# Halved queries, keys and gates in passes 1 to 3 of a fused attention and mixture-of-experts block

## The chip, the cores and the metric

The kernel runs on one core of a Trainium2 chip. The metric is the device time of one execution in microseconds (us). The core has five engines that run side by side, each with an instruction queue of its own: TensorE (PE; its weight loads are shown apart as PEld), VectorE (DVE), ScalarE (ACT), GpSimd (POOL) and SyncE (SP). They meet only through semaphores: an instruction behind a wait stands until the count is reached, and so does all that is behind it in its queue. DMAs are issued from the queues of SP, ACT and POOL.

## The reference

The input `x` is 4 sequences of 512 tokens with 256 features. All is fp32.

```python
mod = (silu(c) @ wmod).reshape(4, 6, 1, 256)        # sa, ca, ga, sb, cb, gb per sequence
h = layernorm(x) * (1 + ca) + sa
q, k, v = h @ wq + bq, h @ wk + bk, h @ wv + bv      # 16 heads of 16
scores = einsum('bhnd,bhmd->bhnm', q, k) * dmask     # gamma ** (n - m) for n >= m
ret = einsum('bhnm,bhmv->bhnv', scores, v)
norm = groupnorm(ret) * gn_w + gn_b                  # per head, over all tokens of a sequence
x = x + ga * ((silu(h @ wg + bg) * norm) @ wo + bo)
h = layernorm(x) * (1 + cb) + sb
w, i = top_k(h @ gate_kernel, 2); w = softmax(w)     # 8 experts, 2 per token
x = x + gb * sum over the two experts of w * ((silu(h @ w0[e]) * (h @ w1[e])) @ wo[e])
```

## The kernel before

**Passes.** The attention part runs as four passes, b = 0 to 3, one for each sequence. Features lie on the 128 partitions in two tiles (ft = 0, 1), the 512 tokens along the free dimension. In pass b the work on sequence b is woven with the rest of its neighbour p = b - 1 (values, group norm, output projection, second layer norm, router, scatter) and, for b >= 2, with the router's results of b - 2. Each engine's order is written out by hand in a loop `for b in range(B)`.

In a pass TensorE does, in this order: the transposes of the normed rows (`turn_x`, issued at the end of the pass before, L1391), queries, keys, values, transposed keys, gates (`project`, L1398, one call for each letter and ft: `q0 q1 k0 k1 g0 g1`), the chunk states (`state_parts`, L1433), the neighbour's output rows (`out_rows`, L1512), the scores (L1451), the product with the states (`from_states`, L1472), the masked scores times values (`values`, L1487), and the transposes of the neighbour's second norm (`turn_h2`, L1522). A `project` call multiplies fp32 weights by the fp32 features `hT`: two matmuls of 128x512, of which each stands in the trace as two records. Its result goes to one of four PSUM banks used in turn (`Ring`, `front_items`); a call waits until the bank's last user has drained it. A second ring of two banks (`tail_items`) serves the neighbour's work. `scores` of set 0 need banks whose last users include the gates, so they wait until ACT has drained them (`gate`, L691 to L696).

ACT drains the features (`features`, L669), queries (L677, L679), keys, gates, applies the group norm (`group_normed`, L703), makes the normed rows (L719), and issues the loads of the experts' weights (`load_expert`, L730, three DMAs of 512 KB each): experts 0 and 1 in pass 0, 2b and 2b + 1 in pass b. In pass 3, `gate(3, 0)` stands behind the wait for `prod_ready`, which DVE gives in `gated` (L1062). DVE also masks the scores (L1023), computes the states and routing tables (`tile_columns`, L1174 to L1194; `table_rows`, L1203). POOL scales `wo` (L552), adds the bias to x (L565), multiplies the decay into the queries (`decay_q`, L530), and scatters the rows to the experts' regions in HBM (L574).

**Steps.** Rows that share an expert are worked on in 39 tiles of 128 (`N_TILES`). The first 8 (`EARLY`) come from a table built from sequences 0 and 1 and run while sequences 2 and 3 are still being routed; for them both up products use fp32 (`up_early`, L1664). From tile 8 on, up products use rounded halves (`up`, L1673 to L1677): the weights and the rows are each split into a part `hi` rounded to fp32r and the rest `lo`, and hi*hi, lo*hi and hi*lo are summed, 6 matmuls of 128x512. Before them TensorE transposes the tile's rows (`turn_rows`, L1580), which SP has fetched (`load_rows`, L439, L460). Tile 8's load also waits for all scatters and for 8 transfers of an empty template (`tmpl`) to the regions' ends (L456), called pads here. SP issues these between the loads of rows 6 and 7. From tile 8 to the end each step repeats with TensorE nearly gapless.

## Time and profile before

| | |
|---|---|
| median of 3 runs | 406.45 us (405.02 to 408.06) |
| the profiled execution's own time | 404.24 us |
| its span in the trace | 402.5 us |
| mean granted TensorE clock | 0.976 of full |
| busy: PE, DVE, POOL, ACT | 362.3, 260.9, 231.4, 173.2 us |

The times of day below are us from the start of the span. Passes 0 to 3 begin with `turn_x` at 11.7, 44.1, 76.4 and 111.4; the last values of pass 3 end at 155.5; the loop from tile 8 on begins at 219.0. "Idle before" is time in which the engine did nothing ahead of an instruction, with what ended it.

### The profile page before, as it was taken

Reading aid. Unit: us, or ns where it says so; the run is one execution under the profiler, and the core shown is the slowest. Engines: PE = TensorE matmul, PEld = TensorE weight load, DVE = VectorE, ACT = ScalarE, POOL = GpSimd, SP = SyncE. Lnnn points to the kernel's source line nnn. Section 1 sums busy time; section 2 is a strip of 40 time slices with the busy share of each in tenths; the row PEclk is TensorE's granted clock in tenths of the full one; section 3 lists DMA queues with packets and bytes.
Section 4 is the critical chain, followed back from the end, with each engine's and each line's share of the span. In section 5 each row is a group of like instructions: output and inputs, shape, how many; then the busy total and the mean of one; then the engine's idle time right before and its main releaser. Section 6 shows DMA issues by size and latency. Waiting matters only on the chain. (4 is left out here: it accounts for less than half of the span.)

```text
span 402.5 us, 11496 instructions
## 1 busy us (share of the span) xinstructions
PE 362.3 (90%) x3893; PEld 271.0 (67%) x3894; DVE 260.9 (65%) x728; ACT 173.2 (43%) x264; POOL 231.4 (57%) x173
## 2 busy tenths in 40 slices
PE   3897899899999798898987999999999999999980
PEld 3474566766766576556644788888888888888860
DVE  6458528755954885757743777777777777777740
ACT  3424336444453313343122255555555555555510
POOL 3112610745781737077375377777777877777851
PEclk9998999999999989899998999999999999999997
DMA  6954090165356442254696333333334343333222
GB/s 220 304 208 161 24 320 4 55 226 209 145 174 229 172 134 69 59 186 146 175 300 151 66 77 72 64 70 75 79 79 79 79 79 79 70 76 62 43 27 25
DMA packets 32322, 49.05 MB, mean 122 GB/s; under 512 B 3198, under 2 KB 18972, under 8 KB 32284
## 3 DMA queue, kind: packets, MB, share of 16 engines
q1 hardware_dynamic: 12968, 19.92, 17.2%
q0 software_dynamic: 8176, 13.65, 15.4%
q10 hardware_dynamic: 11140, 14.96, 10.9%
q8 instruction: 26, 0.43, 0.5%
q14 instruction: 12, 0.10, 0.1%
HBM read 30.35 MB, written 18.16 MB: 121 GB/s over the span
## 5 line engine op out<-in xcount | busy, mean ns | idle before, releaser
L606 POOL TENSOR_TENSOR w_lo<-we,w_hi 128x1024 fp32r<-128x1024 f32 x31 | 76.6, 2471 | 24.3 <-ACT w_hi L813 22.2
L1693 PE MATMUL ps<-we,qeo 128*128 x312 | 75.5, 385 | 1.1 <-ACT qeo L797 0.8
L797 ACT COPY qeo<-ps 128x512 f32<-128x512 f32 x39 | 22.9, 587 | 111.1 <-PE ps L1685 111.1
L1693 PEld LDWEIGHTS ps<-we,qeo 128*128 128x128 f32 x312 | 57.4, 190 | 18.8 <-issue 11.5
L616 POOL DMA_INDIRECT out_dram<-wg_s,qd x30 | 47.0, 1568 | 34.4 <-issue 14.9
L1299 DVE TENSOR_TENSOR w_halves<-we,w_halves 128x1024 fp32r<-128x1024 f32 x31 | 38.0, 1225 | 8.0 <-ACT w_halves L813 8.0
L1271 DVE CAST rT_halves<-ps 128x256 fp32r<-128x256 f32 x31 | 13.2, 425 | 38.2 <-PE ps L1580 38.2
L574 POOL DMA_INDIRECT routed<-h_first,idx x24 | 24.7, 1030 | 16.2 <-DVE idx L1137 9.4
L1664 PE MATMUL ps<-we,xn 128*128 x64 | 33.3, 646 | 0.3 <-issue 0.3
L813 ACT CAST w_hi<-we 128x1024 fp32r x31 | 32.6, 1053 | 0.0
L813 ACT CAST w_halves<-we 128x1024 fp32r x31 | 32.5, 1048 | 0.0
L1279 DVE SCALAR_TENSOR_TENSOR sm<-sm,ps 128x512 f32<-128x512 f32 x39 | 26.5, 679 | 6.2 <-ACT sm L802 6.2
L1673 PE MATMUL ps<-w_halves,rT_halves 128*128 128x512 f32 x62 | 30.2, 487 | 0.0
L1673 PE MATMUL ps<-w_hi,rT_halves 128*128 128x512 f32 x62 | 27.0, 435 | 0.0
L1286 DVE TENSOR_TENSOR sm<-sm,ps 128x512 f32<-128x512 f32 x39 | 26.6, 681 | 0.6 <-PE ps L1664 0.4
L1674 PE MATMUL ps<-w_halves,rT_halves 128*128 128x512 f32 x62 | 24.4, 394 | 0.0
L1674 PE MATMUL ps<-w_hi,rT_halves 128*128 128x512 f32 x62 | 24.4, 394 | 0.0
L802 ACT ACTIVATE sm<-ps 128x512 f32<-128x512 f32 x39 | 23.6, 604 | 0.0
L1685 PE MATMUL ps<-ident,sm 128*128 128x128 f32 x156 | 23.5, 273 | 0.0
L1685 PEld LDWEIGHTS ps<-ident,sm 128*128 128x128 f32 x156 | 19.1, 140 | 6.0 <-issue 1.6
L1023 DVE TENSOR_TENSOR sm<-ps,dmask 128x512 f32<-128x512 f32 x32 | 19.8, 682 | 1.5 <-PE ps L1451 1.4
L1398 PE MATMUL ps<-hT,wq_s 128*128 128x512 f32 x32 | 17.6, 683 | 2.0 <-ACT hT L669 1.8
(237 smaller groups left out, 712.5 us busy)
## 6 DMA issues: line engine op xcount, KB each, us to landing
rowbuf<-routed SPq DMA_DIRECT2D x39, 260.5 KB, 2.9
we<-in_ffn_w_kernel_dram ACTq DMA_DIRECT2D x16, 512.0 KB, 4.3
we<-in_ffn_wo_kernel_dram ACTq DMA_DIRECT2D x8, 512.0 KB, 6.4
routed<-z SPq DMA_DIRECT2D x9, 260.5 KB, 3.3
xs<-in_attn_x_dram SPq DMA_DIRECT2D x4, 512.0 KB, 11.9
out_dram<-xs ACTq DMA_DIRECT2D x4, 512.0 KB, 3.5
we<-in_wmod_dram SPq DMA_DIRECT2D x1, 1024.0 KB, 10.1
sbcb<-gsc_dram SPq DMA_DIRECT2D x4, 256.0 KB, 4.8
```

The source lines that it names most:

```text
L574: g.indirect_dma_start(routed, bass.IndirectOffsetOnAxis(ap=idx[:, k, t:t + 1], axis=0), h2[b][:, t, :], None).then_inc(scattered, 16)
L606: g.tensor_tensor(w_lo[1], expert_up(e, 1), w_hi[1].bitcast(F32), ALU.subtract)\
L616: g.indirect_dma_start(out, bass.IndirectOffsetOnAxis(ap=meta[s % 4][:, TOK - D:TOK - D + 1].bitcast(I32), axis=0), ey[s % 2], None, compu ...
L813: a.copy(w_hi[which], expert_up(e, which)).then_inc(w_hi_ready[which], 1)
L1279: v.scalar_tensor_tensor(out=eth[s % 2], in0=eth[s % 2], scalar=1.0, in1=up_ps[s % 2][0][:, :], op0=ALU.add, op1=ALU.mult).then_inc(in_don ...
L1286: v.tensor_tensor(ein[s % 2], eth[s % 2], up_ps[s % 2][1][:, :], ALU.mult).then_inc(in_done, 1)
L1299: v.tensor_tensor(w_lo[0], expert_up(e, 0), w_hi[0].bitcast(F32), ALU.subtract)\
L1664: last = mm(up_ps[s % 2][which][:, :], rT[s % 2][:, k, :], weights(e, (which * FT + k) * F, F), start=k == 0, stop=k == FT - 1)
L1673: mm(dst, rT_hi[s % 2][:, k, :], w_hi[which][:, k * F:(k + 1) * F], start=k == 0, stop=False)
L1674: mm(dst, rT_lo[s % 2][:, k, :], w_hi[which][:, k * F:(k + 1) * F], start=False, stop=False)
L1685: last = tr(ps[5][:, k * P:(k + 1) * P], ein[s % 2][:, k * P:(k + 1) * P], ident[:, :])
L1693: last = mm(down_ps, eit[s % 2][:, k, :], weights(e, 2 * FT * F + k * D, D), start=k == 0, stop=k == KF - 1)
```

## The change

Queries, keys and gates of passes 1 to 3 (17 of the 18 calls; the last gate, `g1` of pass 3, stays fp32) use the three products of halves. The halves of `wq`, `wk`, `wg` are made once in pass 0: `hi` on ACT, `lo` on POOL behind `add_bias(0)`. The halves of the features are made in each pass: ACT rounds `hT_hi` ahead of `hT`, DVE subtracts (`features_lo`) behind its last masks. They lie in the place of experts 6 and 7, so these experts' loads move behind pass 3's `g0`, ahead of ACT's `gate(3, 0)`. The neighbour's first `values` move ahead of the first query. In pass 3 the table for the early tiles is built later on DVE and TensorE, the loads of rows 0 and 1 move from SP to ACT (`first_rows`, ahead of `second_normed(2)`), and the template and pads move from SP to ACT, spread behind steps 4, 5 and 6. After the passes, DVE does `group_scale` and `gated` of sequence 3 somewhat earlier.

```diff
38.00:42.00 4.00, 3.67 (x135) 0.57 0.03 8 tail_items
+        if b >= 1:
+            items += [(b - 1, n, "dve") for n in ("wo01", "wo23")]
         if b == B - 1:
             items.append((b, "fold", "dve"))
         if b >= 1:
-            items += [(b - 1, n, "dve") for n in ("wo01", "wo23")]
...
38.00:42.00 4.00, 3.67 (x135) 0.57 0.03 8 SP
             sp.wait_ge(tab_ready, 2)
             sp.wait_ge(scattered, SCATTERS * (B - 2))
-            for i in range(EARLY):
-                load_rows(i, i)
+            for i in range(1, EARLY):
+                if i >= 2:
+                    load_rows(i, i)
...
-                if i == 6:
-                    sp.wait_ge(tmpl_ready, 1)
-                    sp.dma_start(routed[PAD_ROW:PAD_ROW + P, :], tmpl).then_inc(tmpl_out, 16)
-                    sp.wait_ge(pad_ready, 1)
-                    for e in range(E):
-                        r = sp.value_load(padi[0:1, e:e + 1], min_val=0, max_val=PAD_ROW - P)
-                        sp.dma_start(routed[bass.ds(r, P), :], tmpl).then_inc(pad_out, 16)
38.00:42.00 4.00, 3.67 (x135) 0.57 0.03 8 POOL, after add_bias(b)
+                if b == 0:
+                    for u, w in enumerate((wq_s, wk_s, wg_s)):
+                        pool.wait_ge(proj_hi_ready, u + 1)
+                        g.tensor_tensor(proj_lo[:, u, :, :], w[:, :, :], proj_hi[:, u, :, :].bitcast(F32),
+                                        ALU.subtract).then_inc(proj_lo_ready, 1)
38.00:42.00 4.00, 3.67 (x135) 0.57 0.03 8 ACT
+            def projection_halves():
+                act.wait_ge(setup_pe, 5)
+                for u, w in enumerate((wq_s, wk_s, wg_s)):
+                    a.copy(proj_hi[:, u, :, :], w[:, :, :]).then_inc(proj_hi_ready, 1)
             def features(b):
+                if b:
+                    for ft in range(FT):
+                        act.wait_ge(front.full, front.filled(b, f"hT{ft}"))
+                        a.activation(hT_hi[:, ft, :], ...).then_inc(ht_hi_ready, 1)
...
+            def first_rows():
+                act.wait_ge(tab_ready, 2)
+                act.wait_ge(scattered, SCATTERS * (B - 2))
+                for i in range(2):
+                    r = act.value_load(tabi[0][0:1, 0, i:i + 1], min_val=0, max_val=PAD_ROW)
+                    act.dma_start(rows[i], routed[bass.ds(r, P), :]).then_inc(row_in[i], 16)
...
38.00:42.00 4.00, 3.67 (x135) 0.57 0.03 8 ACT, the pass
-                if b:
+                if 0 < b < B - 1:
                     load_expert(2 * b)          # and load_expert(2 * b + 1) likewise
...
                 if p >= 0:
                     group_normed(p)
                     act.wait_ge(prod_ready, FT * p + FT)
+                if final:
+                    act.wait_ge(front.full, front.filled(b, "g0"))
+                    act.wait_ge(gb_out, 16)
+                    load_expert(2 * b)
+                    load_expert(2 * b + 1)
                 gate(b, 0)
                 if not final:
                     normed(b + 1)
                     gate(b, 1)
+                if b == 0:
+                    projection_halves()
+                if final:
+                    first_rows()
                 if p >= 0:
                     second_normed(p)
...
-            run_steps(act, act_step, first=3)
+            act_step(3, 3)
+            act_step(4, 4)
+            act.wait_ge(tmpl_ready, 1)
+            act.dma_start(routed[PAD_ROW:PAD_ROW + P, :], tmpl).then_inc(tmpl_out, 16)
+            pads(range(0, 3))
+            act_step(5, 5)
+            pads(range(3, 6))
+            act_step(6, 6)
+            pads(range(6, E))
+            run_steps(act, act_step, first=7)
38.00:42.00 4.00, 3.67 (x135) 0.57 0.03 8 DVE
+            def features_lo(b):
+                for ft in range(FT):
+                    dve.wait_ge(ht_ready, FT * b + ft + 1)
+                    v.tensor_tensor(hT_lo[ft][:, :], hT[:, ft, :], hT_hi[:, ft, :].bitcast(F32), ALU.subtract)\
+                        .then_inc(ht_lo_ready, 1)
...
                 if last:
-                    tile_columns(0)
+                    tile_starts(0)       # the first of its instructions
                 if p >= 0:
                     gated(p)
...
                 if last:
-                    table_rows(0)
+                    tile_columns(0)
                 gates(b, 0)
...
                 if p >= 0:
                     attention_out(p)
+                if last:
+                    table_rows(0)
...
                 masks(b, 1)
+                if not last:
+                    features_lo(b + 1)
38.00:42.00 4.00, 3.67 (x135) 0.57 0.03 8 DVE, after the passes
+            group_scale(b)
             choose_places(b - 1)
-            group_scale(b)
             choose_weights(b - 1)
             take_rows(1, 1)
+            gated(b)
             silu_mul(0, 0)
-            gated(b)
             hidden(0, 0)
38.00:42.00 4.00, 3.67 (x135) 0.57 0.03 8 PE
+            def project_halves(b, w, u, ft):
+                n = f"{w}{ft}"
+                wait(pe, front.free(b, n))
+                if b == 1:
+                    pe.wait_ge(proj_lo_ready, u + 1)
+                dst, cols = front.bank(b, n)[:, :], slice(ft * P, (ft + 1) * P)
+                for k in range(FT):
+                    mm(dst, proj_hi[:, u, k, cols], hT_hi[:, k, :], start=k == 0, stop=False)
+                    mm(dst, proj_lo[:, u, k, cols], hT_hi[:, k, :], start=False, stop=False)
+                pe.wait_ge(ht_lo_ready, FT * b)
+                for k in range(FT):
+                    last = mm(dst, proj_hi[:, u, k, cols], hT_lo[k][:, :], start=False, stop=k == FT - 1)
+                last.then_inc(front.full, 1)
...
-                wait(pe, front.drains(b, "hT1"))
-                project(b, "q", wq_s, 0)
+                if p >= 0:
+                    values(p, 0)
+                    pe.wait_ge(ht_hi_ready, FT * b)
+                else:
+                    wait(pe, front.drains(b, "hT1"))
+                query(b, 0)
                 if p >= 1:
                     router(p - 1)
-                if p >= 0:
-                    values(p, 0)
...
                 if final:
                     scores(b, 0, range(PAIRS))
-                    fold(0)
...
                 scores(b, 1, (2, 3))
                 if final:
+                    fold(0)
                     values(b, 0)
```

## Rows read from the trace of the kernel before

**Rows 1.** The page: busy time, share of the span and instructions by engine.
```profile
PE 362.3 (90%) x3893; PEld 271.0 (67%) x3894; DVE 260.9 (65%) x728; ACT 173.2 (43%) x264; POOL 231.4 (57%) x173
```

**Rows 2.** Timeline of TensorE, pass 1: start, length, line, tiles, count, idle before.
```profile
46.23 1.98 PE L1398 MATMUL ps<-hT,wq_s 128*128 128x512 f32 x4 [1.00 <-ACT hT L669]
48.15 1.48 PE L1487 MATMUL ps<-sm,vx 64*32 64x64 f32 x128
49.56 1.98 PE L1398 MATMUL ps<-hT,wq_s 128*128 128x512 f32 x4
51.38 1.88 PE L1398 MATMUL ps<-hT,wk_s 128*128 128x512 f32 x4
...
57.04 0.39 PE L1497 MATMUL ps<-gmv,blkavg 128*128 128x4 f32 x2
```

**Rows 3.** The chain of waits, one matmul of halves in a loop step.
```profile
226.61 0.23 PE ps L1673
```

**Rows 4.** Timeline of POOL at the start of pass 1.
```profile
46.87 2.36 POOL L565 TENSOR_TENSOR xs<-xs,ga_bc 128x1024 f32<-128x1024 f32 x1
49.18 1.27 POOL L530 TENSOR_TENSOR qd<-parts,qdec 128x512 f32<-128x512 f32 x1
```

**Rows 5.** TensorE by stretches: length, busy, granted clock, DMA share, GB/s.
```profile
34.70:37.06 2.36, 0.02 (x1) 1.00 0.36 121
38.00:42.00 4.00, 3.67 (x135) 0.57 0.03 8
```

**Rows 6.** Timeline of TensorE, the end of pass 3.
```profile
138.78 1.35 PE L1451 MATMUL ps<-qeo,kT 32*64 32x128 f32 x64 [2.72 <-ACTq L696]
...
149.01 0.79 PE L1487 MATMUL ps<-sm,vx 64*32 64x64 f32 x56
...
151.47 1.09 PE L1522 MATMUL ps<-ident,h_first 128*128 128x128 f32 x8
...
155.44 0.44 PE L1580 MATMUL ps<-ident,rowbuf 128*128 128x128 f32 x2
```

**Rows 7.** Timeline of ACT and its DMA queue, pass 0, then pass 3.
```profile
22.73 0.91 ACTq L730 DMA_DIRECT2D we<-in_ffn_w_kernel_dram  x2
...
25.30 0.49 ACTq L730 DMA_DIRECT2D we<-in_ffn_wo_kernel_dram  x1
...
137.33 0.69 ACT L691 ACTIVATE z<-ps,vcol 128x512 f32<-128x512 f32 x1 [4.04 <-DVE sm L1062]
...
149.33 0.60 ACT L719 ACTIVATE h_first<-xs,nmr,rs 128x256 f32<-128x256 f32 x1 [10.74 <-POOL nmr L518]
...
209.50 0.60 ACT L802 ACTIVATE sm<-ps 128x512 f32<-128x512 f32 x1
```

**Rows 8.** Timeline of DVE, pass 3, the table and the product with the gates.
```profile
133.93 0.15 DVE L1180 TENSOR_TENSOR enc<-stc,tls 8x1 f32<-8x1 f32 x1
...
136.00 1.29 DVE L1062 TENSOR_TENSOR sm<-sm,z 128x512 f32<-128x512 f32 x2
```

**Rows 9.** Timeline of TensorE, its three longest waits among the early tiles.
```profile
167.41 3.69 PE L1512 MATMUL ps<-wob,sm 128*128 128x256 f32 x16 [1.38 <-issue]
...
210.44 0.44 PE L1580 MATMUL ps<-ident,rowbuf 128*128 128x128 f32 x2 [1.47 <-DMA rowbuf<-routed]
...
219.01 0.69 PE L1580 MATMUL ps<-ident,rowbuf 128*128 128x128 f32 x2 [2.53 <-DMA rowbuf<-routed]
```

**Rows 10.** Timeline of SP's DMA queue: the eight pads.
```profile
196.10 8.91 SPq L456 DMA_DIRECT2D routed<-z  x8
```

**Rows 11.** The chain of waits ahead of the loop: start, length, what.
```profile
211.82 3.28 DMA routed<-h_last,idx
215.35 0.38 SPq L436
```

**Rows 12.** The page's DMA issues: count, KB each, us to landing.
```profile
we<-in_ffn_wo_kernel_dram ACTq DMA_DIRECT2D x8, 512.0 KB, 6.4
routed<-z SPq DMA_DIRECT2D x9, 260.5 KB, 3.3
```

61 lines of the change are left out of this document (43 added, 18 removed).

## The prediction

> **What bounds the kernel now.** I read the page's busy line first: TensorE is busy for 90% of the span, the next engine for 65% [rows 1]. TensorE's timeline then shows where it is not. From tile 8 on it is nearly gapless, so whatever is won or lost before 219.0 shifts the end by as much, and nothing in the change alters a loop step. Before that, TensorE waits at a few places, and each has another cause: ACT's late drain of the gate in pass 3 [rows 6], the product with the gates of sequence 3, and the fetched rows of tiles 7 and 8 [rows 9]. The chain of waits of the page starts at the last of these: last scatter, its landing, SP's step towards tile 8's load [rows 11]. Therefore I go through the stages one by one, and ask in each who is last.
>
> **The saving on TensorE.** An fp32 call takes 51.38 - 49.56 = 1.82 us [rows 2]. A halved call is 6 matmuls at 0.23 us each [rows 3], 1.38 us, and I add 0.12 for the start of a group: 1.50. That is 0.32 a call, and for 17 calls 5.4 us. It counts where TensorE is last.
>
> **Pass 1.** Before, the first query starts at 46.23 after a wait of 1.00 for the features, so TensorE was done with the transposes at 45.2 [rows 2]. Now the values of sequence 0 (49.56 - 48.15 = 1.41) fill that gap, to 46.6. But the first query also waits for POOL's `lo` of `wq`. POOL waits for statistics of DVE first, and its bias addition ends at 46.87 + 2.36 = 49.2 [rows 4]; the change moves nothing of this forward. One 128x512 operation of POOL takes 1.27 [rows 4], so the `lo` is there at 50.5 and TensorE stands for 3.9 us. ACT's `hi` and DVE's two subtractions are long done (both engines are free there) and cost nothing. `lo` of `wk` and `wg` come at 51.8 and 53.0, in time; the `decay_q` behind them is 3.8 late, which is less than the way to the chunk states, the first to want it. In pass 0 TensorE did almost nothing for 2.36 us, and in the 4 us from 38 on its granted clock was 0.57 in the mean, that is mostly the lower level of 1.2 GHz [rows 5]: 4 x (1 - 0.57) = 1.7 us of work lost. I take the same here, since the new gap is longer than that one. From 50.5, four calls of 1.50, values 1.41, 0.25 for a small stall that stands there now, and 1.7 for the clock give 59.9 where `average` started at 57.04 [rows 2]: **2.8 us lost**. Bounds: 1.1 lost if the clock holds; 4.5 if it falls twice. The two gates then save 0.64: DVE, which waits for TensorE there now and then, follows.
>
> **Pass 2.** From the first transposes done, ACT's four activations of about 0.6 and DVE's last subtraction, with the hops between, want some 3.3 us. TensorE has the other transposes (0.5), `turn_h2` (1.0), the values (1.4) and two of the three products of the query (0.9) meanwhile, 3.8: covered. If that cover fails, it costs at most 1 us in each of passes 2 and 3. Six calls save 1.9; the neighbour's statistics on DVE come about 0.2 late. **1.7 won.**
>
> **Pass 3.** Five calls save 1.6 up to the gate, of which DVE's chain passes on 1.5. `gated` moves 2.0 us forward besides, because the table's columns (133.93 to 136.00) leave its way [rows 8]. But between `gated` and `gate(3, 0)` ACT now issues six DMAs for experts 6 and 7. In pass 0 the same six took 22.73 to 25.79, 3.1 us [rows 7]. Net the gate comes 0.4 earlier than at 137.33, and the wait of 2.72 before the scores grows to about 3.8 while TensorE's saved work is lost in it; the low clock after it stays as it is. Scores, output rows, states and scores again follow, without the fold 0.6 earlier, so to 148.4 instead of 149.01 [rows 6]. Fold and table end at 149.0. Then ACT reads two table entries and issues rows 0 and 1 before it may norm sequence 2: SP's pads, each a read of the table and a DMA, followed each other at (8.91 - 0.33) / 7 = 1.23, with 0.33 the length of one issue [rows 10]; two are 2.4. Norming starts at 151.5 instead of 149.33 [rows 7], `turn_h2` at 153.6 instead of 151.47, and with 1.0 and 1.4 behind it the pass ends at 156.0 instead of 155.44 [rows 6]: **0.6 lost.** Bounds: 1.2 won, if a stall of 1.25 in the last values falls into the new wait and the reads are quicker; 2.5 lost, if the 3 MB of weights, now beside eight scatters, slow these. The weights themselves must be there at 156; issued by 137 they have 19 us, where one of them took 6.4 to land [rows 12].
>
> **Early tiles.** `gated` ahead of tile 0's activation removes the 1.38 before the output rows [rows 9]. POOL's scatters of sequence 2 then start 0.7 earlier, and POOL passes on only that. Row 7's load was issued behind the pads, which ended at 205.0 [rows 10]; with the pads on ACT it is early and the 1.47 goes. What is late next is row 8. It needs the last scatter and also the last pads, which ACT issues behind the activation of step 6 at 209.50 [rows 7]: less 0.7, plus two reads and issues less the 0.33 of the last (2.1), plus 3.3 to land [rows 12], 214.2 against the 215.1 at which the scatters were in [rows 11]. So the loop starts **0.9 earlier**, with a wait of 3.5 us where 2.53 was. Bounds: 2.7, if the scatters, no longer beside a crowd of pads, set it; 0.5 lost, if the pads land 1.4 later.
>
> The Trainium skill says (DMA: Bandwidth & Descriptors, Issuing engines are not separate DMA queues) that issuing from several engines saves only sequencer time, usually small beside the transfer. By that rule moving pads to ACT would be worth nothing. The trace disagrees in size: 8.9 us of SP's queue went to eight pads [rows 10]; it agrees that this is not where row 8's wait comes from.
>
> **Sum**: 2.8 - 0.64 - 1.7 + 0.6 - 0.9 = +0.2 us. The profiled execution took 404.24, which is 2.2 below the median of 406.45. On the median this is 406.6.
>
> **Rivals.**
> A. TensorE is last nearly everywhere. Then 5.4 us of calls come through, and with 1.38 and 1.47 8.3 us: 398. With the stall in pass 1 but without its clock loss, and with the better bounds of pass 3 and of row 8, the sum is +0.2 - 1.7 - 1.8 - 1.8 = -5.1: 401.3. For it: TensorE's 90%. Against it: POOL's 49.2, which the change doesn't touch. The range of this case is 398 to 402.4. The Trainium skill (Trace Analysis, Identifying the Most-Contended Engine) would have the busiest engine eased first, which is this case; the trace bears it out for pass 2 only. Chance 0.25.
> B. Slower. One mechanism: the weights of experts 6 and 7 are issued in pass 3 at 134 to 137, while POOL is still scattering sequence 1. If they hold the scatters' landing beyond 149, then `first_rows`, the norm of sequence 2, and through them every later routing step slip. It decides from a delay of about 4 us on, by my estimate of when the scatters are in, one landing of 3.3 [rows 11] behind the last issue at about 141. Each further us goes to the end; 4 us more give 410.6 to 412. Against it: the weights' 3 MB went in pass 3 before in DMAs of the same size at 6.4 us a landing [rows 12], with the scatters a second stream of 2 MB. Chance 0.12.
> C. The halves aren't faster in a single call: TensorE pays fp32 time for them. Then 5.4 less saved, of which some 2.5 count: 409 to 411. Rows 3 speak against it. Chance 0.03, over the bound in a third of it.
> D. The forecast, within its own range of 403 to 410: 0.60.
>
> **Numbers.** I call a change of over 1%, 4.1 us, faster or slower; that is about what a measurement of this kernel tells from none. Faster (below 402.4): all of A, and 0.02 of D. Slower (over 410.5): B, 0.01 of C, 0.02 of D. Rounded: 0.27, 0.58, 0.15. Range for 8 in 10: 400.5 to 410.0, which leaves a third of A and most of B outside.
>
> **What would show it.** In the trace after: the first query of pass 1 starts at about 50.5, with some 4 us idle before it that a POOL subtraction ends, and a stretch at half clock behind it; calls of 1.4 to 1.5 us; `average` of pass 1 near 60; the wait before pass 3's first scores between 3 and 4.5 us, ended by ACT; `turn_h2` of sequence 2 waits for ACT; no wait before row 7, over 3 us before row 8, ended by a load that waited for pads. I am wrong if the wait in pass 1 is under 2 us, if the clock stays full behind it, or if row 8's wait is gone.

## The result, and the profile after

The changed kernel takes 425.25 us, median of 4 runs (424.21 to 428.34); the kernel before took 407.25 on the same chip (405.02 to 408.38). The ratio is 1.0486, interval 1.0419 to 1.0554: slower, where the prediction had 406.6 and a range up to 410.0. The profiled execution spans 422.9 us against 402.5.

Two notes on the change. In its diff above, each part is headed by the name of an engine or a list (`SP`, `ACT`, `DVE`, ...); the row of the clock that stands in front of that name is no part of the change. And one move is not in that diff: in step 3 TensorE's `rank(3)` stands before the down product instead of before the second up product.

The page's busy line comes first. It answers to [rows 1].

```profile
PE 365.3 (86%) x3927; PEld 284.5 (67%) x3928; DVE 273.6 (65%) x734; ACT 180.0 (43%) x273; POOL 236.9 (56%) x176
```

TensorE was to have 5.4 us less work. It is busy for 3.0 us more, and idle for 17 us more. DVE is busy for 12.7 us more, with only 6 more instructions. So neither the saving nor the price of DVE's part came as foreseen. Where the 20.4 us lie is read from TensorE's landmarks in the two timelines (`average` of pass 1, 2 and 3, the first turned rows of tiles 0 and 8, the end):

| stage | before | after | difference |
|---|---|---|---|
| start to `average` of pass 1 | 57.04 | 60.70 | +3.7 |
| to `average` of pass 2 | 34.55 | 39.25 | +4.7 |
| to `average` of pass 3 | 35.83 | 41.48 | +5.65 |
| to row 0 (end of pass 3) | 28.02 | 33.54 | +5.5 |
| row 0 to row 8 | 63.57 | 63.75 | +0.2 |
| loop | 183.5 | 184.2 | +0.7 |

Little is lost in the early tiles and the loop (0.9 us together); the four stretches before row 0 lose 3.7 to 5.65 each.

The stages of one execution are only roughly those of the kernel. The kernels e3, e4 and e5 below run the same code in passes 2 and 3, up to `average` of pass 3. They take 79.5, 81.4 and 76.8 us for both passes together, where this trace has 80.7 and the kernel before 70.4. Pass 2 alone takes 36.3 in e4 and e5 instead of 39.25, and pass 3 takes 45.1 in e4. So the sum of the two passes is what can be compared.

**Pass 1.** Timeline of TensorE, which answers to [rows 2], and under it POOL's, which answers to [rows 4]: start, length, line, tiles, count, and in brackets the idle time before with what ended it.

```profile
51.65 0.76 PE L1475 MATMUL ps<-hT_hi,proj_hi 128*128 128x512 f32 x1 [4.95 <-POOL proj_lo L599]
52.21 0.63 PE L1476 MATMUL ps<-hT_hi,proj_lo 128*128 128x512 f32 x1
52.64 0.63 PE L1475 MATMUL ps<-hT_hi,proj_hi 128*128 128x512 f32 x1
...
55.02 0.40 PE L1475 MATMUL ps<-hT_hi,proj_hi 128*128 128x512 f32 x1
55.25 0.39 PE L1476 MATMUL ps<-hT_hi,proj_lo 128*128 128x512 f32 x1
```

```profile
46.95 2.89 POOL L565 TENSOR_TENSOR xs<-xs,ga_bc 128x1024 f32<-128x1024 f32 x1
49.80 1.71 POOL L599 TENSOR_TENSOR proj_lo<-wq_s,proj_hi 128x512 fp32r<-128x512 f32 x1
```

The wait for POOL's `lo` is there, 4.95 us instead of 3.9. The bias addition took 2.89 where it took 2.36, and a subtraction 1.71 where the prediction had 1.27 from POOL's other operation of that size: 1.0 us between them. The matmuls behind the wait start 0.43 apart and, from 55.02 on, 0.23 apart: the first were at half clock.

**DVE's subtractions** are the new work on that engine. Its timeline, passes 1 to 3:

```profile
46.95 0.69 DVE L1065 TENSOR_TENSOR hT_lo<-hT,hT_hi 128x512 fp32r<-128x512 f32 x1 [1.17 <-ACT hT L685]
47.83 2.55 DVE L1065 TENSOR_TENSOR hT_lo<-hT,hT_hi 128x512 fp32r<-128x512 f32 x1 [0.20 <-ACT hT L685]
...
82.45 4.70 DVE L1065 TENSOR_TENSOR hT_lo<-hT,hT_hi 128x512 fp32r<-128x512 f32 x2 [1.17 <-ACT hT L685]
...
122.30 4.59 DVE L1065 TENSOR_TENSOR hT_lo<-hT,hT_hi 128x512 fp32r<-128x512 f32 x2 [1.50 <-ACT hT L685]
```

One of them takes 0.69. The others take 2.55, and 4.70 and 4.59 for two. Compare the first pair with POOL's rows above. POOL's addition, which reads two tiles, starts at 46.95 together with DVE's first subtraction, and becomes 0.5 longer. DVE's second starts at 47.83, inside that addition, and ends at 50.38, which is 0.54 behind the addition's end at 49.84; POOL's next one, which starts at 49.80, becomes 0.44 longer. So the two engines do not share: one stands until the other's instruction is over. The Trainium skill says just that (SBUF — State Buffer, SBUF: two separate sides): the pair of ports is "an **exclusive lock**, not a bandwidth split", held for a whole instruction, by a DVE operation with two SBUF inputs against a POOL operation that reads SBUF. The trace agrees. In passes 2 and 3 the pair of subtractions lies beside a multiplication and an addition of 128x1024 on POOL (81.82 to 86.60, 121.56 to 126.34), and TensorE waits:

```profile
87.20 0.72 PE L1479 MATMUL ps<-hT_lo,proj_hi 128*128 128x512 f32 x2 [3.00 <-DVE hT_lo L1065]
...
99.95 0.39 PE L1586 MATMUL ps<-gmv,blkavg 128*128 128x4 f32 x2 [0.93 <-DVE gmv L1095]
...
126.95 1.22 PE L1479 MATMUL ps<-hT_lo,proj_hi 128*128 128x512 f32 x2 [1.68 <-DVE hT_lo L1065]
...
141.43 0.39 PE L1586 MATMUL ps<-gmv,blkavg 128*128 128x4 f32 x2 [1.17 <-DVE gmv L1095]
```

**The clock.** TensorE by stretches, as in [rows 5]: stretch, its length, busy us (count) of PE, PEld, DVE, ACT and POOL, granted clock, DMA share, GB/s.

```profile
50.50:55.00 4.50, 3.35 (x8) 2.69 (x9) 0.00 (x0) 0.42 (x1) 3.48 (x3) 0.62 0.01 4
88.00:95.00 7.00, 7.00 (x27) 5.94 (x27) 3.19 (x24) 4.22 (x7) 2.37 (x2) 0.57 0.66 228
126.00:136.00 10.00, 9.05 (x29) 7.87 (x30) 4.08 (x25) 4.05 (x7) 2.67 (x3) 0.52 0.01 2
153.00:160.00 7.00, 4.95 (x71) 4.11 (x72) 3.73 (x9) 1.27 (x2) 1.91 (x2) 0.56 1.05 398
235.00:242.00 7.00, 3.28 (x6) 1.73 (x7) 2.52 (x5) 1.68 (x2) 3.94 (x2) 0.55 0.51 103
```

Each stretch at about 0.5, the lower level of 1.2 GHz, begins in or just behind one of the waits shown: 4.95, 3.00, 1.68, 5.59 and 5.31. Over the span the mean granted clock is 0.976 before and 0.944 after, so 402.5 x 0.024 = 9.7 us of full-clock time are missing before and 422.9 x 0.056 = 23.7 after. This is 14 us of the 20.4, though not all of it need be on the path. TensorE is 90 to 100% busy in the stretches at 88 and 126, and does there in 7 and 10 us what would take some 4 and 5.2 at full clock (7 x 0.57 and 10 x 0.52).

A long wait is not the only thing a low stretch can follow. In e4 and e5 one begins at 79.0 and 80.5, behind waits of 0.55 and 0.4 us only: `turn_x` takes 1.94 instead of 1.17. There TensorE comes to DVE's subtractions late, waits 0.75 and 0.70 for them instead of 3.00, and has no low stretch behind that wait.

**Pass 3.** Timelines of ACT with its queue, and of TensorE, answering to [rows 6, 7].

```profile
149.27 0.90 ACTq L750 DMA_DIRECT2D we<-in_ffn_w_kernel_dram  x2
...
152.93 0.62 ACTq L750 DMA_DIRECT2D we<-in_ffn_wo_kernel_dram  x1
153.60 0.69 ACT L709 ACTIVATE z<-ps,vcol 128x512 f32<-128x512 f32 x1 [6.30 <-issue]
...
167.35 1.45 ACTq L763 DMA_DIRECT2D rowbuf<-routed  x2
169.20 0.60 ACT L737 ACTIVATE h_first<-xs,nmr,rs 128x256 f32<-128x256 f32 x1 [14.34 <-issue]
```

```profile
155.05 2.02 PE L1540 MATMUL ps<-qeo,kT 32*64 32x128 f32 x64 [5.59 <-ACTq L714]
157.00 5.49 PE L1601 MATMUL ps<-wob,sm 128*128 128x256 f32 x16
...
171.33 1.97 PE L1611 MATMUL ps<-ident,h_first 128*128 128x128 f32 x8 [2.71 <-ACT h_first L737]
```

The six issues take 4.3 us, where 3.1 was predicted, and the scores wait for 5.59 where 2.72 stood and 3.8 was predicted. The output rows behind it take 5.49, at half clock. So they did before (5.41 behind the wait of 2.72; at full clock the same 16 matmuls took 3.69 in [rows 9]), but the low stretch is longer now: 153.5 to 161 where it was 140.5 to 144. ACT drains the gate 12.2 us behind `average`, where it was 9.9. The norm of sequence 2 waits for `first_rows`, as predicted.

**Row 8.** The chain of waits (start, length, what) and TensorE, answering to [rows 9, 11].

```profile
229.89 4.53 DMA routed<-z
...
236.00 2.68 DMA rowbuf<-routed
```

```profile
238.72 0.69 PE L1669 MATMUL ps<-ident,rowbuf 128*128 128x128 f32 x2 [5.31 <-DMA rowbuf<-routed]
```

A pad is last now, as predicted; it took 4.53 to land instead of 3.3. The wait is 5.31 instead of 2.53, yet the stage is only 0.2 longer, in part because the wait before row 7 (1.47) is gone.

### The profile page after: what moved, and what is told of

The parts are those of the page before. It is cut to its first block, busy times and chain, and to the rows that moved or that the text cites. A ratio compares the mean times of both kernels' runs of the same rounds, so it can differ in the third digit from the quotient of the medians.

```text
span 422.9 us, 11605 instructions
## 1 busy us (share of the span) xinstructions
PE 365.3 (86%) x3927; PEld 284.5 (67%) x3928; DVE 273.6 (65%) x734; ACT 180.0 (43%) x273; POOL 236.9 (56%) x176
## 4 chain that ended last, share of the span: by engine, by line
PE 41%; DMA 4%; DVE 3%; issue 2%; POOL 2%; ACT 1%; POOLq 1%; ACTq 0%; SPq 0%; DVEq 0%
PE ps L1785 13%; PE ps L1766 6%; PE ps L1765 6%; PE ps L1769 6%; PE ps L1777 3%; PE ps L1756 3%; DMA out_dram<-wg_s,qd 2%; PE ps L1669 2%; DMA routed<-z 1%; POOL routed L574 1%; DMA out_dram<-wg_s,wv_s 1%; DMA rowbuf<-routed 1%; ACT h_last L737 0%; DVE vd L1148 0%; POOLq L130 0%
## 5 line engine op out<-in xcount | busy, mean ns | idle before, releaser
L1785 PEld LDWEIGHTS ps<-we,qeo 128*128 128x128 f32 x312 | 57.4, 190 | 20.1 <-issue 13.0
L1756 PE MATMUL ps<-we,xn 128*128 x64 | 31.9, 622 | 0.4 <-issue 0.4
L530 POOL TENSOR_TENSOR qd<-parts,qdec 128x512 f32<-128x512 f32 x8 | 9.5, 1184 | 25.6 <-ACT parts L695 16.9
L1475 PE MATMUL ps<-hT_hi,proj_hi 128*128 128x512 f32 x34 | 17.7, 520 | 4.9 <-POOL proj_lo L599 4.9
```

Source lines behind the costliest of these rows:

```text
L1756: last = mm(up_ps[s % 2][which][:, :], rT[s % 2][:, k, :], weights(e, (which * FT + k) * F, F), start=k == 0, stop=k == FT - 1)
L1785: last = mm(down_ps, eit[s % 2][:, k, :], weights(e, 2 * FT * F + k * D, D), start=k == 0, stop=k == KF - 1)
```

## The experiments

Ratios are to the kernel before on the same chip, with a 95% interval. "Stage" times are from each kernel's profiled execution, by the landmarks above.

### e1_alone and e2_psum: DVE's subtractions without POOL beside them

In the first, POOL waits for DVE's subtractions of the next pass before it modulates. In the second DVE takes one input from PSUM: it scales the transposed features again and takes `hi` off in the same instruction, without the bias `saT` that `hi` has.

```diff
                 if p >= 0:
+                    if b < B - 1:
+                        pool.wait_ge(ht_lo_ready, FT * (b + 1))
                     modulate(p)
```

```diff
-                    v.tensor_tensor(hT_lo[ft][:, :], hT[:, ft, :], hT_hi[:, ft, :].bitcast(F32), ALU.subtract)
+                    v.scalar_tensor_tensor(out=hT_lo[ft][:, :], in0=front.bank(b, f"hT{ft}")[:, :],
+                                           scalar=ca1T[:, ft, b:b + 1], in1=hT_hi[:, ft, :].bitcast(F32),
+                                           op0=ALU.mult, op1=ALU.subtract)
```

> Theory P: a DVE subtraction of two SBUF tensors stands still while POOL works on SBUF tensors, so the pair of subtractions takes 4.6 to 4.7 us instead of about 1.3 in passes 2 and 3 (pairs at 82.45 and 122.30 of the changed kernel). Here POOL waits for the pair before it starts the neighbour's two modulations; nothing else is changed. P: the pair takes 1.4 us or less in passes 2 and 3, TensorE's waits of 3.00 and 1.68 before the third product go, and with them the low clock behind them (about 1.7 us of work each). Together 6 to 9 us faster than the changed kernel. Rival Q: the subtraction is slow by its fp32r output or by its operands. Then the pair stays at 4.6 and POOL's later modulation makes the time the same or 1 to 3 us longer. The Trainium skill (GPSIMD Engine Reference, 8. Key points) says that GpSimd shares its SBUF interfaces with VectorE and contends with DVE instructions that have two SBUF inputs; that is P.

> The subtraction takes the transposed rows from PSUM (scaled, less the rounded half) in place of the SBUF copy, so that DVE has one SBUF input; POOL keeps its order. It leaves out the added shift in the small half. P in its narrow form (two SBUF inputs are what collides): the pair takes about 1.4 us though POOL works beside it, gain 6 to 10 us over the changed kernel, pass 1's included. P in a wide form (any DVE operation that reads SBUF stands still beside POOL): the pair stays at 4 us or more. Q: 4.6 as well.

Measured: 417.84 us, 1.0211 [1.0162, 1.0261], and 417.25 us, 1.0190 [1.0119, 1.0260]. Both take 2.6 to 2.8% off the changed kernel's 1.0486. On the same chip e3 and e4, which keep the collision, took 426.14 and 423.91, 6 to 9 us more. DVE's timelines, first of e1_alone, then of e2_psum:

```profile
82.72 0.69 DVE L1067 TENSOR_TENSOR hT_lo<-hT,hT_hi 128x512 fp32r<-128x512 f32 x1 [1.74 <-ACT hT L687]
83.61 0.69 DVE L1067 TENSOR_TENSOR hT_lo<-hT,hT_hi 128x512 fp32r<-128x512 f32 x1 [0.20 <-ACT hT L687]
...
118.77 0.69 DVE L1067 TENSOR_TENSOR hT_lo<-hT,hT_hi 128x512 fp32r<-128x512 f32 x1 [1.72 <-ACT hT L687]
```

```profile
81.58 1.64 DVE L1065 SCALAR_TENSOR_TENSOR hT_lo<-ps,modT,hT_hi 128x512 fp32r<-128x512 f32 x2 [1.17 <-ACT hT L685]
```

Alone, a subtraction takes 0.69; with one input in PSUM it takes 0.82 even beside POOL, whose operations are not held up either (2.19 and 2.19 at 80.97 and 83.23, where the changed kernel has 2.20 and 2.50). Two different edits with nothing else in common give the same gain, so the collision is shown as the cause of this part. TensorE's waits of 3.00 and 1.68 for `hT_lo` are gone, and the stages of passes 2 and 3 are 35.8 and 36.4 (e1), 37.1 and 36.1 (e2), where 39.25 and 41.5 stood. What is left of the loss after it, some 2%, lies for the most part in pass 1 (60.4 and 59.8 against 57.0) and in the stretch to row 0 (33.6 and 33.3 against 28.0). In e2, where pass 1 is free of the collision too, the wait before the first query is 3.95 and the query starts at 50.65.

### e3_weights_early: `proj_lo` of the weights early on POOL

```diff
                     for later in range(1, B):
+                        if later == B - 1:
+                            for u, w in enumerate((wq_s, wk_s, wg_s)):
+                                pool.wait_ge(proj_hi_ready, u + 1)
+                                g.tensor_tensor(proj_lo[:, u, :, :], w[:, :, :], ...)
                         first_scale(later)
```

> POOL makes the small halves of the three weights before it waits for the last of the first norm's statistics, where it is idle (38.6 to 43.4), in place of behind the bias addition. Theory S: the wait of 4.95 before the first query of pass 1 and the low clock behind it come from this order alone. Then the query starts at about 48 (third product at the latest when DVE's second subtraction is done at about 50, if that still stands beside the bias addition), and the kernel is 4 to 6 us faster than the changed one. Rival: TensorE then waits for the DVE subtraction beside the bias addition instead; the wait shrinks to 2 to 3 us, low clock stays, gain 2 to 3 us.

Measured: 426.14 us, 1.0393 [1.0309, 1.0477]. The interval overlaps that of the changed kernel, so neither the 4 to 6 us of the theory nor the 2 to 3 of the rival are seen. POOL's wait is gone from TensorE's timeline, but DVE's is behind it:

```profile
51.89 1.22 PE L1479 MATMUL ps<-hT_lo,proj_hi 128*128 128x512 f32 x2 [1.85 <-DVE hT_lo L1065]
```

`average` of pass 1 comes at 61.3 rather than 60.7: `turn_x` of sequence 1 now waits 2.11 for DVE. Taking a wait away won nothing while the next stood behind it.

### e4_gate_first: loads of experts 6 and 7 behind the gate

```diff
                 if final:
-                    load_expert(2 * b)
-                    load_expert(2 * b + 1)
-                gate(b, 0)
+                gate(b, 0)
+                if final:
+                    load_expert(2 * b)
+                    load_expert(2 * b + 1)
```

> In pass 3 ACT drains the first gate before it issues the six loads of experts 6 and 7, not behind them. In the changed kernel the issues took 149.27 to 153.55 and TensorE stood 5.59 before the scores. Theory L: these issues are the wait. The gate comes 4.3 us earlier, TensorE's wait falls to about 1.3, and the kernel is 3 to 4.5 us faster, if nothing else is last. Rival: the scores come earlier but the low clock, the table and the norm of sequence 2 behind first_rows hold the rest, and only 1 to 2 us reach the end.

Measured: 423.91 us, 1.0353 [1.0289, 1.0416]. By the ratios this is 1.3% better than the changed kernel, with intervals that just do not meet. Timeline of TensorE:

```profile
151.02 0.66 PE L1541 MATMUL ps<-qeo,kT 32*64 32x128 f32 x22 [1.25 <-ACTq L714]
...
159.70 0.94 PE L1562 MATMUL ps<-qd,parts 32*32 32x64 f32 x43 [1.55 <-issue]
165.98 1.83 PE L1577 MATMUL ps<-sm,vx 64*32 64x64 f32 x110 [1.92 <-issue]
```

The wait before the scores fell from 5.59 to 1.25, and the stretch to row 0 from 33.5 to 30.9. But 3.5 us of waits stand there now that no engine is seen to end ("issue"), in the states and the values. This one execution spans 422.7 us, no less than the changed kernel's 422.9: pass 3 up to `average`, which the edit does not touch, took 45.1, and row 0 to row 8 took 65.6. More on these "issue" waits stands under e16_pads_left below.

### e7_all_mended and e5_pads_sp: several waits at once, and the pads on SP

e7_all_mended is the changed kernel with the edits of e1 and e3, the loads **behind** the gate as in e4, all pads issued by SP behind row 7's load, and rows 0 and 1 loaded by SP. Its expectation as recorded says that experts 6 and 7 stay ahead of the gate; the kernel that ran has them behind it. e5_pads_sp is the changed kernel with the pads alone on SP behind row 7.

```diff
-            pads(range(0, 3))      # ACT, and so on to E
+            # SP, behind row 7's load
+            for e in range(E):
+                r = sp.value_load(padi[0:1, e:e + 1], min_val=0, max_val=PAD_ROW - P)
+                sp.dma_start(routed[bass.ds(r, P), :], tmpl).then_inc(pad_out, 16)
```

> Four waits taken out together: POOL modulates behind DVE's subtractions, POOL makes the weights' small halves ahead of the last statistics, experts 6 and 7 stay ahead of the gate as in the changed kernel, the pads go back to SP but behind row 7's load, and rows 0 and 1 go back to SP. Theory W (each wait has its own cause and they add up): 6.6 for the subtractions (measured), 2 to 4 for the weights, 2 for rows 0 and 1, 3 to 5 for the pads, so about 410 to 414 where the changed kernel has about 428 on this chip. Theory C (the granted clock): the changed kernel has 12 low stretches of 3.4 us against 4 before, each worth 1.7 us of work, and the runs so far removed waits without removing low stretches; then this one stays above 415 unless the stretches go too, and the time above the kernel before is about 1.7 us for each stretch above 4.

> The changed kernel with the template and the pads issued by SP behind the load of row 7, no pads on ACT. Row 8 was waited for 5.31 us, its load released by the last pad, which landed 4.5 us after its issue. Theory R: pads that ACT may only issue behind step 6 are what is late. Then they land before the last scatter, the wait before row 8 falls to 2.5 to 3.5, and 2 to 3 us are won. Rival: the last scatter is no earlier than the pads, or the table's read; then the wait stays over 4.5 and the time within 1 us.

Measured: e7 412.14 us, 1.0188 [1.0113, 1.0262]; e5 426.20 us, 1.0524 [1.0444, 1.0603]. e7 is better than the changed kernel by 2.8%, no more than e1 alone. Of its stages pass 1 is 58.9 (2 us above before), passes 2 and 3 are 35.5 and 37.0 (1 us above each) and the stretch to row 0 is 30.0 (2 above). e7 came out where the theory of independent waits put it (410 to 414), and below the 415 that its rival set. The pads where they stand in e5 did not help: its interval overlaps that of the changed kernel. Chains of waits of e5, then e7: the last scatter of sequence 3.

```profile
229.28 5.94 DMA routed<-h_last,idx
```

```profile
215.23 6.32 DMA routed<-h_last,idx
```

It landed in 3.28 before [rows 11]. SP issues eight pads in one burst there, just as the last scatters are under way, and row 8 waits for the scatter.

### e11_mended_pads_back: e7 with the pads at their old place

> The kernel with the waits taken out (POOL modulates behind DVE's subtractions, weights' small halves early, the loads of experts 6 and 7 behind the gate, rows 0 and 1 on SP), but the pads are issued by SP between rows 6 and 7 as in the kernel before, not behind row 7. There the pads ran beside the scatters, and the last scatter took 6.3 us to land where it took 3.28 before. If the pads' place did that, it lands in about 3.3, and the kernel is 2 to 3 us faster than that one: ratio to before about 1.012. If other transfers did it, within 1 us of 1.019. By the stages it can't come under 1.0: passes 2 and 3 stay about 1 us longer than before each although TensorE computes 1.9 us less in each.

The edit puts the pads of e7 between the loads of rows 6 and 7, on SP, as before the change. Measured: 411.05 us, 1.0117 [1.0014, 1.0219]. The last scatter lands in 4.21, and row 0 to row 8 takes 63.3 instead of e7's 64.0. The wait before row 7 is back with 1.93. The intervals of e7 and e11 overlap, so the pads' place is not shown to be worth time. So even with the collision, POOL's wait, the gate and the pads mended, the halves win nothing over the kernel before.

### e8_filled and e13_filled_more: TensorE kept busy over the waits

e8 is the changed kernel with extra matmuls of halves, without use, before the first query: 20 in pass 1, 12 in pass 2, 8 in pass 3. Their results are overwritten. e13 adds six fp32 matmuls before pass 3's first scores and six before row 8.

```diff
                 dst, cols = front.bank(b, n)[:, :], slice(ft * P, (ft + 1) * P)
+                for _ in range((0, 20, 12, 8)[b] if n == "q0" else 0):
+                    mm(dst, proj_hi[:, u, 0, cols], hT_hi[:, 0, :], start=True, stop=True)
                 if b == 1:
                     pe.wait_ge(proj_lo_ready, u + 1)
```

> The changed kernel, but TensorE multiplies on while it would wait: 20, 12 and 8 matmuls of 128x512 of halves into the bank of the first query of passes 1, 2 and 3, overwritten by the query itself (about 4.6, 2.8 and 1.9 us at full clock). Theory C, by waits: the low stretches at 51, 88 and 126 of the changed kernel (six of 3.4 us) follow the waits of 4.95, 3.00 and 1.68 before them; with these filled they go, and the kernel is 6 to 10 us faster though it computes more. Rival: the clock falls for another reason (what TensorE computes, not that it waits); then the stretches stay and the kernel is 0 to 3 us slower.

> The changed kernel with the first queries filled as in the filled one (20, 12 and 8 matmuls), and 6 fp32 matmuls of 128x512 each (5.1 us at full clock) in place of the waits of 5.3 to 5.6 before pass 3's scores and before row 8. Theory C, by waits: the low stretches at 144 and 230 (6.8 each) go too, and 3 to 6 us more are won than by the first filling, since each 3.4 at half clock costs 1.7. Rival: the chain of DVE and POOL is last there, so the stretches go but only the one before the loop (3.4 to 6.8 us of it run in the loop itself) is worth anything, 1 to 3 us.

Measured: e8 422.01 us, 1.0412 [1.0347, 1.0478], its profiled span 417.4 against 422.9; e13 417.01 us, 1.0289 [1.0230, 1.0349]. These kernels do more work than the changed one. e8 alone is not clear of noise: it gained less than the 6 to 10 us expected, and its interval overlaps that of the changed kernel. e13's does not. e8's TensorE over the stretches that were at half clock:

```profile
50.50:55.00 4.50, 4.50 (x22) 3.72 (x21) 1.64 (x1) 1.18 (x2) 4.44 (x4) 1.00 0.02 7
88.00:95.00 7.00, 6.20 (x154) 5.18 (x154) 5.75 (x35) 3.78 (x7) 2.43 (x2) 1.00 0.94 329
126.00:136.00 10.00, 8.06 (x161) 6.36 (x161) 8.62 (x51) 4.77 (x8) 2.44 (x2) 1.00 0.10 29
```

All three are at 1.00. DVE's subtractions are as long as before, so the collision is not what is changed here, yet passes 2 and 3 together take 75.1 us, in e8 and in e13, where the four traces of the same code without filling have 76.8 to 81.4. With e13's ratio, the clock is thus shown as a cost of its own, one that work in the waits takes away. In e13 the stretch before the loop is at full clock as well, and the loop takes 182.4 instead of 184.2. But its stretch from 156 to 172 has a mean clock of 0.57, for 16 us:

```profile
156.00:172.00 16.00, 11.47 (x323) 8.63 (x316) 4.93 (x14) 3.63 (x6) 9.58 (x7) 0.57 0.31 92
```

Filling one wait did not keep the clock up behind the next.

### e9_no_halves: the moves alone

All projections are fp32 calls again; `hi` and `lo` are neither formed nor used, and every move stays.

```diff
-                project_halves(b, "q", 0, ft) if b else project(b, "q", wq_s, ft)   # k and g likewise
+                project(b, "q", wq_s, ft)
```

> All of the change but the halves: queries, keys and gates in fp32 as before, none of the halves made, while the values go first, the loads of experts 6 and 7 stand before the last gate, ACT fetches rows 0 and 1 and writes the pads. If the halves carry the loss (subtraction, weights, clock), this is within 4 to 6 us of the kernel before: gate and first_rows cost 3 to 4, the pads 1 to 3. If the moves carry it, it is 8 us slower or more.

Measured: 412.58 us, 1.0160 [1.0088, 1.0232]. So the halves net cost 1.0486 / 1.0160 = 3.2%, and the moves 1.6%. With the collision taken out, e1 is only 1.0211 / 1.0160 = 0.5% above e9, which is within the intervals: nearly all of what the halves cost is the collision and what follows from it. Stages: pass 1 is back (57.4), to row 0 is not (33.3). Timeline of TensorE:

```profile
143.94 2.02 PE L1525 MATMUL ps<-qeo,kT 32*64 32x128 f32 x64 [5.47 <-ACTq L703]
```

### e10_table_later, e12_values_first, e14_both_moves: two moves by themselves

All three start from the kernel **before**. e10 has the table's columns and rows and its fold later, and `group_scale` and `gated` earlier; e12 has the values of sequence p ahead of the first query; e14 has both.

```diff
                 if last:
-                    tile_columns(0)
+                    tile_starts(0)
                 if p >= 0:
                     gated(p)
...
                 if last:
-                    table_rows(0)
+                    tile_columns(0)
                 gates(b, 0)
```

```diff
+                if p >= 0:
+                    values(p, 0)
                 wait(pe, front.drains(b, "hT1"))
                 project(b, "q", wq_s, 0)
                 if p >= 1:
                     router(p - 1)
-                if p >= 0:
-                    values(p, 0)
```

> The kernel before with one part of the change alone: in pass 3 DVE computes the table's columns behind the states and its rows behind attention_out, TensorE's fold stands behind the scores, and after the passes group_scale and gated come earlier. No halves, and loads, rows and pads as before. Theory W: the wait of 2.72 before pass 3's scores, which ended with ACT's gate behind DVE's gated, shrinks by 2.0, the low stretch behind it goes (1.7), and the wait of 1.38 before sequence 3's output rows goes: 2 to 4 us faster than before. Rival K (the routing chain of DVE and POOL from the last values to tile 8's row is last, 63 to 64 us in each kernel that ran so far): only what comes ahead of the last values counts, 1 to 3 us.

> The kernel before with one part of the change alone: the neighbour's first values stand ahead of the first query. The router comes 1.4 us later, so DVE's choice of experts, the ranks, the second values and the group statistics behind it come later too. Theory D (these, not TensorE's work, are last in passes 2 and 3, since each kernel of the change waits 0.9 to 1.2 for the statistics before average): pass 2 takes 1 to 2 us longer, pass 3 0.5 to 1, pass 1 0.5 less; 1 to 2.5 us slower. Rival: the values cover the wait for the features (1.0 in pass 1) and nothing waits for the router: 0 to 1 us faster.

> The kernel before with two of the moves together: the table later and the product with the gates earlier, and the values of sequence p ahead of the first query. If the parts add, 0.990 x 0.999 = 0.989 of before, about 402 us. Theory (the queue moves cost): under 0.993, so that e9_no_halves' 1.016 is made of what this kernel lacks. Rival (the two moves hurt each other: the values' move takes TensorE's cover from where the table's move makes DVE later): 1.000 or more.

Measured: e10 402.31 us (14 runs), 0.9902 [0.9860, 0.9945]; e12 404.45 (10 runs), 0.9986 [0.9940, 1.0031]; e14 402.21 (5 runs), 0.9883 [0.9818, 0.9949]. e10 and e14 beat both kernels; e10 alone accounts for the gain. (e10's profiled execution took 408.89 us, 1.6% above its median, so its stages are not compared.) In e14's trace the wait of 2.72 before the scores is down to 0.67, and that of 1.38 before sequence 3's output rows is gone, the two waits that this move was to take. e12 explains the values. Its time did not move, where 1 to 2.5 us more were expected, but its stages went as its theory says. Its `average` of pass 1 is at 55.3, 1.7 earlier, and the stretches after it are 1.2 and 0.8 longer. Timeline of TensorE:

```profile
91.06 0.39 PE L1497 MATMUL ps<-gmv,blkavg 128*128 128x4 f32 x2 [0.93 <-DVE gmv L1037]
...
127.68 0.38 PE L1497 MATMUL ps<-gmv,blkavg 128*128 128x4 f32 x2 [1.18 <-DVE gmv L1037]
```

The same 0.93 and 1.17 stand before `average` in the changed kernel. With the values first, the router and the DVE work that it releases come later, and the group statistics are last for TensorE. In passes 2 and 3 they, not TensorE's calls, set the time. The two passes together say the same: 72.4, 72.4 and 72.7 us with fp32 calls (e9, e12, e14), and 72.2, 72.5 and 72.9 with halves and without the collision there (e1, e7, e11), where the kernel before has 70.4. All six have the values first. Whether halves would gain with the values in their old place, no run shows.

### e15_loads_left and e16_pads_left: which of the moves onto ACT's queue costs

e9_no_halves is 1.016 and e14_both_moves 0.988, so 2.8% lie in what else was moved: experts 6 and 7, rows 0 and 1, the pads, and `rank(3)` in step 3. e15 is e9 with pads and first rows on SP as before; the loads stay ahead of the gate. e16 is e9 with the loads behind the gate and the first rows on SP; the pads stay on ACT.

```diff
 e15:
-                if final:
-                    first_rows()
-            pads(range(0, 3))      # and so on: back to SP, between rows 6 and 7
 e16:
-                if final:
-                    first_rows()
                 gate(b, 0)
+                if final:
+                    load_expert(2 * b)
+                    load_expert(2 * b + 1)
```

> e9_no_halves with the pads back on SP between rows 6 and 7 and rows 0 and 1 loaded by SP; of the moves onto ACT's queue only the loads of experts 6 and 7 between the product with the gates and the last gate are left. Theory (the loads' 4.3 us ahead of the gate cost about 1%, 3 to 4 us of the wait before the scores): 1.000 to 1.005. Rival (they are covered, the pads are what costs): 0.990 as e14_both_moves.

> e9_no_halves with the loads of experts 6 and 7 behind the last gate and rows 0 and 1 loaded by SP; the pads stay on ACT as in the changed kernel. Theory (the pads come late on ACT and row 8 waits for them, 4.84 in e9_no_halves against 2.53 before): 1.000 to 1.005, row 8's wait 4.5 to 5 us. Rival (row 8 is set by the scatters' chain whoever issues the pads): 0.990 as e14_both_moves, wait under 3.5.

Measured: e15 408.58 us (11 runs), 1.0043 [1.0003, 1.0083]; e16 408.60 (11 runs), 1.0068 [1.0029, 1.0106]. e15 came out where its theory put it, and e16 just above (1.000 to 1.005 was expected), but for e16 the theory was wrong all the same. By stages:

| stage | e14 | e15 | e16 |
|---|---|---|---|
| `average` of pass 3 | 130.66 | 129.50 | 130.56 |
| to row 0 | 25.4 | 32.0 | 31.6 |
| row 0 to row 8 | 64.3 | 63.1 | 64.0 |

The pads on ACT are not what costs: row 0 to row 8 takes 64.0 with them and 64.3 and 63.1 without, though the wait before row 8 is 4.16, and the intervals of e15 and e16 overlap. Both kernels lose over 6 us before row 0, where the loads are issued, whether ahead of the gate or behind it. `rank(3)` comes behind row 0 and has no part in that. TensorE by stretches, first of e15 ahead of the gate, then of e16 behind it, and e16's timeline; e14 has a DMA share of 0.21 from 148 to 152.

```profile
142.00:148.00 6.00, 4.35 (x70) 3.60 (x71) 2.98 (x5) 1.27 (x2) 1.36 (x2) 0.50 1.04 374
```

```profile
148.00:152.00 4.00, 2.00 (x67) 1.93 (x70) 1.50 (x9) 0.00 (x0) 2.23 (x3) 0.90 1.03 385
152.00:156.00 4.00, 1.83 (x66) 0.99 (x61) 2.71 (x6) 2.08 (x4) 3.33 (x3) 0.50 0.96 313
156.00:160.00 4.00, 4.00 (x128) 3.38 (x127) 0.00 (x0) 1.50 (x2) 0.61 (x1) 0.50 0.48 137
```

```profile
150.00 0.34 PE L1545 MATMUL ps<-qd,parts 32*32 32x64 f32 x6 [2.31 <-issue]
...
156.00 1.34 PE L1560 MATMUL ps<-sm,vx 64*32 64x64 f32 x74 [2.17 <-issue]
```

Ahead of the gate, the issues hold it back (a wait of 5.52 before the scores, then half clock). Behind it, the gate is in time (a wait of 0.66), and 3 MB land while TensorE goes through some 300 small matmuls. There it stands twice for over 2 us, each time in the middle of one call that has no wait inside it in the program: between 106 and 6 of the 112 matmuls with the states, and between 54 and 74 of 128 for the values. In e14, with the same matmuls and a DMA share of 0.21 at 148 to 152, no such stop is over 0.8. Behind the stops, again, comes the lower clock.

What stops TensorE there stays open. Stops of the same kind also stand where there is hardly any traffic: 1.25 us between 48 and 80 matmuls of one call in the kernel before (DMA share 0.00 from 153 to 154.5), and 1.96 us in e8 (share 0.12 from 157.5 to 159.4). The profile shows a queue of kind "instruction" on the same 16 DMA engines, so one reading is that TensorE waits for its own instructions behind other traffic. But that queue moved 0.07 MB from 140 to 162 in e16 and in e14 alike, and no run here tests it. What is shown is that the loads in this place cost some 6 us before row 0; by way of these stops is argued.

## Why the prediction was wrong

**DVE's subtractions, the main fault.** The step read: "DVE's two subtractions are long done (both engines are free there) and cost nothing", and for passes 2 and 3 "covered. If that cover fails, it costs at most 1 us". Two take 4.7 beside POOL instead of 1.4, two times the 0.69 of one alone. The missed row was in the trace of before. There POOL's work already held DVE back. Its timelines of DVE and of POOL:

```profile
185.34 1.79 DVE L1090 TENSOR_TENSOR vd<-mx 128x4 f32<-128x4 f32 x1
...
187.73 1.67 DVE L1096 CAST ixf<-ix 128x8 f32<-128x8 uint32 x1
```

```profile
184.33 2.77 POOL L541 TENSOR_TENSOR h_last<-h_last,sbcb 128x1024 f32<-128x1024 f32 x1
187.18 2.18 POOL L544 TENSOR_TENSOR h_last<-h_last,sbcb 128x1024 f32<-128x1024 f32 x1
```

That is 4 elements a partition in 1.79 us, beside a POOL operation; it ends with it (187.13 and 187.10). At 160.19, where POOL is idle, the same instruction takes 0.17. The cast, which has one input in SBUF, also ends with POOL's addition (189.40 and 189.36); where POOL is idle, at 92.08 in the changed kernel's trace, it takes 0.17. So a second SBUF input is not the only form that waits. The bound of 1 us came from counting durations, and did not ask what runs on POOL at that moment. e1 and e2 put the price at 2.6 to 2.8% of the changed kernel: 11 to 12 us by the ratios, 6 to 9 against e3 and e4 on the same chip, 6.4 to 7.0 by the profiled spans.

**The clock behind new waits.** I took 1.7 us, once, in pass 1. The low stretches after it cost about that (50.5 to 55: 4.5 x 0.38 = 1.7). But behind each further wait, of 3.00, 1.68 and 5.59, stood one too, of 3.0, 4.8 and 3.1 us lost (length times one minus clock, from the rows above); only the last had one before, of 1.7. A clock cost was put on the one wait that I expected, and the upper ends of the range had none for the waits that a failing cover would bring. e8 and e13 show that these are a cost of their own.

**Pass 1**: 2.8 lost predicted, 3.7 measured. The mechanism was right (POOL's `lo`, then half clock); the wait was 4.95 rather than 3.9, by the collision. Without it, in e2, the wait is 3.95, the query starts at 50.65 (50.5 predicted) and `average` comes at 59.8 (59.9 predicted).

**The saving in passes 2 and 3.** "1.7 won" in pass 2 was wrong by more than the collision. e12 shows that there TensorE is not last before `average`: with 1.7 us won in pass 1, it gives 2.0 back in passes 2 and 3. With the values first, as in the change, it is the group statistics that TensorE waits for, and halves and fp32 calls take the same time (72.2 to 72.9 and 72.4 to 72.7 for both passes). And e11, with most of the new waits mended, is still 1.0117. In [rows 3] a halved matmul costs 0.23; at full clock it does here too (55.02 to 55.25), and a call from one start to the next takes 1.49 (68.31 to 69.80), where 1.50 was predicted and an fp32 call takes 1.82. So rival C is out. The calls are shorter; their time isn't last.

**Pass 3**: 0.6 lost predicted; the stretch from `average` of pass 3 to row 0 lost 5.5. Of the step "Net the gate comes 0.4 earlier", the first half holds: counted from `average`, DVE's product with the gates starts 2.1 us earlier (6.5 us behind it instead of 8.6), and by itself this move is a gain (e10, 0.9902). The issues ahead of the gate take it away: the gate comes 2.3 us later, counted in the same way. Two sizes were wrong: 4.3 for the issues instead of 3.1, and nothing for the clock ("the low clock after it stays as it is"), which behind the longer wait stayed low for 7.5 us instead of 3.5. That is 1.7 us more lost. I priced the loads as time on ACT's queue alone; e15 and e16 put them at 1.6 to 1.9% (1.0043 and 1.0068 over 0.9883; `rank(3)` is in this too, and in e16 the pads), wherever they stand around the gate. The halves need this move: `proj_hi`, `hT_hi` and the others lie in the buffers of experts 6 and 7. So this is part of the price of the halves, and not of a separate choice. `first_rows` was right: 2.71 before `turn_h2`.

**Early tiles**: 0.9 won predicted, 0.2 lost. Row 7's wait went, row 8's grew beyond 3.5 to 5.31 with a pad last, as foreseen; the pad landed in 4.53 instead of 3.3. "`gated` ahead of tile 0's activation removes the 1.38" did not hold in this execution of the changed kernel (1.35 with "issue" in TensorE's timeline), but did in e14, and e3, e4 and e5 have 0.17 there. Row 0 to row 8 took 63 to 66 us in every kernel tried, and waits there trade places. That a chain of routing on DVE and POOL sets it is argued from this alone.

**Rivals.** A (TensorE last everywhere) is refuted by e12 and e11. B named the loads of experts 6 and 7, and pass 3 was the place, but by way of the scatters' landing: the norm of sequence 2 waited for `first_rows`, which issued its loads at 167.35, 1.1 us behind the table's last step on DVE (166.22), while POOL had issued its last scatter by 155.3. It had 0.12. That its time of 410.6 to 412 is nearly that of the moves alone (412.58) is luck. What none of the cases held was the collision on DVE.

**What stays open**: what the "issue" waits are; whether halves gain with the values behind the first query; what `rank(3)`'s later place in step 3 is worth (it is in e9, e15 and e16, and was not tried alone); and why e11 still stands 1 point above before, of which the loads' move may be all.

## What to carry to other kernels

Before a cost is put on DVE work, above all with two inputs in SBUF, look which POOL operations run in the same microseconds, in the trace of before: a 0.69 us operation can take 2.5. Price every new wait of TensorE together with the low clock that can follow it (here 1.7 to 4.8 us each in one execution, though the stretches do not fall in the same place in each), and ask of each saved call whether TensorE is last at the next joint, since a call that isn't last saves nothing. Test the parts of a bundle apart: here a reordering that was only an accompaniment gained 1% by itself, and the main part lost 3%.
